# GpSimd joins the four score minima of a step, and evictions three and four carry on the minimum of one and two

## What is computed

```
q, k = fq_sym(q * scale, axis=-1), fq_sym(k, axis=-1)   # 8 bits per row
v = fq_sym(v, axis=2)                                   # 8 bits per column
attn = softmax(q @ k.T)                                 # per head, 1600 x 5776
attn = round(attn / s) * s, s = max(attn) / 255         # 8 bits per row
x = x + (attn @ v) @ Wp + bp
x = x + ffn(layernorm(x))                               # w13 (2816 x 512), w2 (512 x 1408)
```

## Time and profile before

| | us |
|---|---|
| median of three runs (1844.59 to 1848.37) | 1847.6 |
| the profiled execution | 1847.68 |
| its span | 1845.9 |
| VectorE busy | 1691.0 (92%) |
| TensorE matmuls busy | 1631.2 (88%) |
| ScalarE busy | 1391.7 (75%) |
| GpSimd busy | 1375.3 (75%) |
| evictions of 1536 and 1168 columns, mean of one | 1.81 and 1.42 |
| the join of the minima, mean of one | 0.16 |

### The profile page before, as it was taken

One profiled execution on the slowest core, in us unless ns is written; L12 is line 12 of the kernel. 1 busy time (PEld: TensorE's weight loads), 2 busy tenths in 40 slices (PEclk: granted clock), 3 DMA queues, 4 the chain that ended last, 5 costly groups with the idle time before them and its releaser, 6 DMA issues.

```text
span 1845.9 us, 41823 instructions
## 1 busy us (share of the span) xinstructions
PE 1631.2 (88%) x17032; PEld 1153.6 (62%) x17032; DVE 1691.0 (92%) x2670; ACT 1391.7 (75%) x1362; POOL 1375.3 (75%) x759
## 2 busy tenths in 40 slices
PE   7997899989888888888898898888889888789998
PEld 6884666666566666655566666555555555478876
DVE  6869999999999999999999999999999999986665
ACT  2446898888988898889888988897888888742232
POOL 1432789898879888888898889887898798753232
PEclk9999999999999999999999999999999999989999
DMA  5578988998899899989998998889888998732221
GB/s 175 193 224 201 209 187 177 184 196 166 181 186 198 176 193 184 187 164 177 191 200 177 181 196 170 158 158 181 168 169 157 205 185 160 166 116 45 67 58 47
DMA packets 851530, 309.96 MB, mean 168 GB/s; under 512 B 784966, under 2 KB 813964, under 8 KB 851212
## 3 DMA queue, kind: packets, MB, share of 16 engines
q1 hardware_dynamic: 851340, 307.29, 81.0%
HBM read 74.26 MB, written 39.59 MB: 62 GB/s over the span
## 4 chain that ended last, share of the span: by engine, by line
DVE 57%; PE 21%; issue 9%; POOL 7%; DMA 5%; ACT 1%; SPq 1%; POOLq 0%; DVEq 0%; ACTq 0%
DVE S L1295 51%; PE PS L876 5%; POOL PT L1529 5%; PE PK L913 3%; DMA PP<-Pr 3%; PE PS L743 2%; PE PK L682 2%; PE PK L684 2%; PE PS L711 2%; DVE MJ L1321 1%; PE PO L684 1%; DVE kam L1186 1%; PE PO L682 1%; DVE VMX L1190 1%; PE PO L762 1%
## 5 line engine op out<-in xcount | busy, mean ns | idle before, releaser
L1295 DVE TENSOR_SCALAR_CACHE_REDUCE S<-PS,SQN 128x1536 f32<-128x1536 f32 (+1 forms) x768 | 1283.2, 1714 | 20.5 <-PE PS L743 10.1
L1529 POOL CAST PT<-PP 128x3072 uint16<-128x3072 uint8 (+1 forms) x400 | 1048.5, 2650 | 223.6 <-DMA PP<-Pr 217.7
L1088 ACT ACTIVATE Pr<-S,MS 128x5888 uint8<-128x5888 f32 x200 | 1041.2, 5206 | 166.7 <-DVE MJ L1321 140.0
L743 PE MATMUL PS<-KT,QT 96*128 96x512 bf16 (+1 forms) x2496 | 633.4, 373 | 153.2 <-DVE S L1295 140.0
L762 PEld LDWEIGHTS PO<-VI,PT 128*128 128x128 f16 x9200 | 338.4, 96 | 199.6 <-issue 31.3
L743 PEld LDWEIGHTS PS<-KT,QT 96*128 96x128 bf16 (+1 forms) x2496 | 191.5, 99 | 364.9 <-DVE S L1295 131.1
L762 PE MATMUL PO<-VI,PT 128*128 128x32 bf16 x9200 | 356.3, 178 | 20.1 <-ACT AO L1038 9.7
L684 PE MATMUL PK<-CT,WG 128*128 128x128 f32 (+1 forms) x1288 | 212.7, 293 | 7.0 <-DMA CT<-ctxt 7.0
L682 PE MATMUL PK<-WG,CT 128*128 128x128 f32 (+1 forms) x1288 | 210.7, 293 | 6.3 <-ACT VF L949 3.7
L684 PEld LDWEIGHTS PK<-CT,WG 128*128 128x128 f32 x1288 | 169.1, 194 | 10.0 <-issue 7.8
L682 PEld LDWEIGHTS PK<-WG,CT 128*128 128x128 f32 (+1 forms) x1288 | 167.0, 192 | 8.5 <-issue 6.6
(11 more groups left out here) (156 smaller groups left out, 1538.0 us busy)
## 6 DMA issues: line engine op xcount, KB each, us to landing
CT<-ctxt SPq DMA_DIRECT2D x180, 256.0 KB, 3.2
k_rows<-KS SPq DMA_DIRECT2D x39, 512.0 KB, 4.0
q_rows<-QS SPq DMA_DIRECT2D x13, 512.0 KB, 4.6
W13F<-w13T SPq DMA_DIRECT2D x12, 352.0 KB, 3.7
PP<-Pr SPq DMA_TRANSPOSE x200, 6.0
XT<-x SPq DMA_DIRECT2D x12, 256.0 KB, 4.4
XR<-x SPq DMA_DIRECT2D x12, 256.0 KB, 3.3
base_rows<-XO SPq DMA_DIRECT2D x12, 256.0 KB, 3.3
```

The source lines that it names most:

```text
L743: last = pe.matmul(PS[n % 2][p0:p0 + r, f:f + w], QT[h % 3][0:PARTS * HD, q0:q0 + r], KT[h % 3][0:PARTS * HD, c * CHUNK + f:c * CHUNK + f ...
L1088: act.activation(Pr[i % 2].rearrange("p t q b -> p t b q"), S[i % 2].rearrange("p (t b q) -> p t b q", b=2, q=P), ACT.Exp, bias=MS[:, i % ...
L1295: v.tensor_scalar(S[i % 2][:, c * CHUNK:c * CHUNK + CW[c]], PS[n % 2][:, 0:CW[c]], neg_step, None, ALU.mult, ALU.min, accum_out=MN[:, i % ...
L1529: gp.tensor_copy(PT[i % 2][:, 2 * t0:2 * t1, :].rearrange("p (t b) q -> p t b q", b=2), PP[i % 2][:, t0:t1, :].bitcast(U8).rearrange("p t ...
```

## The change

The join leaves VectorE. Evictions three and four take as second scalar the minimum that eviction one or two left (`MN[:, i % 2, c - 2:c - 1]`), which seeds the running minimum, so that columns 2 and 3 of `MN` cover all four chunks. GpSimd takes the smaller of these two columns and adds ln 255 in one operation on 128x1, `offset(i)`, which signals `s_mx` in place of the join. Evictions three and four wait for the end of the eviction two before them. `offset(i)` is due at i + 0.25 in `todo`: ahead of `unpack(i - 2, 0)` at i + 0.3, and behind all that is due up to i + 0.25. It waits for all four evictions of step i.

```diff
-        MJ = sb("MJ", [P, NC_], F32)
...
                     v.wait_ge(M["s_qk"], n + 1)
 
-                    v.tensor_scalar(S[i % 2][:, c * CHUNK:c * CHUNK + CW[c]], PS[n % 2][:, 0:CW[c]], neg_step, None,
+                    if c >= 2:
+                        v.wait_ge(M["s_ev"], n - 1)
+                    least = MN[:, i % 2, c - 2:c - 1] if c >= 2 else None
+                    v.tensor_scalar(S[i % 2][:, c * CHUNK:c * CHUNK + CW[c]], PS[n % 2][:, 0:CW[c]], neg_step, least,
                                     ALU.mult, ALU.min, accum_out=MN[:, i % 2, c:c + 1]).then_inc(M["s_ev"], 1)
...
-                v.wait_ge(M["s_ev"], NC_ * (i + 1))
-
-                v.tensor_scalar(MJ[:, :], MN[:, i % 2, :], LN255, None, ALU.add, ALU.min,
-                                accum_out=MS[:, i % 2, 0:1]).then_inc(M["s_mx"], 1)
...
+            def offset(i):
+
+                gp.wait_ge(M["s_ev"], NC_ * (i + 1))
+                gp.tensor_scalar(MS[:, i % 2, 0:1], MN[:, i % 2, 3:4], MN[:, i % 2, 2:3], LN255, ALU.min,
+                                 ALU.add).then_inc(M["s_mx"], 1)
+
...
             todo += [(i + 2.3 + 0.4 * part, unpack, (i, part)) for i in range(NA) for part in range(NCAST)]
+            todo += [(i + 0.25, offset, (i,)) for i in range(NA)]
```

## The result

The changed kernel takes 1876.1 us (median; 1872.1 to 1878.7), the kernel before, run beside it on the same chip, 1847.9 us. The ratio is 1.0148, with a 95% interval of 1.0130 to 1.0166. The forecast was 1850 with a range to 1862. The median stands 4 us over this execution, the fastest of its kernel.

A forecast was written before the change was run, and what follows sets the result against it. VectorE's own instructions were taken to bound the attention phase; 46 us removed less 24 (seeds), 2, 4.5, 3, 6.5 (group changes), 2.5 (TensorE-paced steps) and 6 gave -2.5, so 1850 us; 8-in-10 range 1838 to 1862.

The forecast's parts named there:

- The tail: After the last step, casts waiting for the last offset delay w13's high parts and VectorE's last subtraction: 6 us lost.
- batches: Slots with two key operations on GpSimd (36 batches): only those four steps apart lose, 0.1 us each, 2 us.
- normalises: GpSimd's normalise, 2.1 us more in a slot, delays the exponential behind key operations: 4.5 us together.
- splits: Splits of w13 on GpSimd, 16 slots in two runs of eight, 6.98 against 6.69 us a slot: 3 us.
- TensorE's values for i-4 read casts made two slots before: hidden.: In plain slots, casts held behind the offset were claimed to cost TensorE's value products nothing.
- 2.7 late: Normalise behind two key operations (steps 54 and 104): exponential 2.7 us late, VectorE stalled 1.8 us.
- rival 1: GpSimd's queue costs more, through late exponentials: typically 8 to 12 us slower, 1858; chance 0.37 together with rival 3.
- It stalls VectorE up to 1.5 us: At three head-group changes, ScalarE's rounding of V waits for a cast behind an offset: 1 us each after partial absorption.
- Slack 0.9 us: In each step, how late the exponential could be before VectorE needs its score buffer: 0.9 us free.
- Rival 2: The slack absorbs GpSimd's queue: 10 us faster, 1837.5, or 1841 with half of the other terms; chance 0.25.
- Rival 3: Casts set the pace, so VectorE's time is worth nothing: some 1860 us; folded into rival 1, joint chance 0.37.
- The result hardly depends on the seed: Were seeds free on VectorE, other engines would take up the difference: 2 us faster instead of 2.5 slower.

The follow-up runs named there:

- the run without a join: Changed kernel with no GpSimd operation for the offset and no join anywhere, seeds kept, exponential taking column 3 of the minima as bias: 1831.5 us, ratio 0.9910.
- the run with the last offset moved: Changed kernel with only the last step's offset moved behind the two casts of step 197: 1869.6 us, ratio 1.0116.
- the run with the queue wait: Kernel before, join kept and no seeds, plus an unread one-column GpSimd operation at the offset's place with its wait: 1862.7 us, ratio 1.0077.
- a second operation: Changed kernel with another one-column GpSimd operation behind each offset, its result read by nobody: 1906.2 us, ratio 1.0323.
- the offset between the casts: Changed kernel with the offset of step i due at i + 0.5, between the two casts of step i-2: 1963.7 us, ratio 1.0624.
- the pair above: Changed kernel with normalises moved to slots without key operations (1865.1 us), and that with last offset and V casts moved too (1861.6 us), compared at steps 38 to 40.
- one copy on ScalarE: Changed kernel without GpSimd's operation; ScalarE copies the last minimum as bias ahead of each exponential, omitting the two-way minimum and ln 255: 1838.0 us, ratio 0.9943.

## Why the prediction was wrong

**What held.** The sign was right and the size wrong by a factor of ten: 2.5 us slower forecast, 28 measured. The removal (0.23 us a step: 6.92 with seeds and join, 6.69 with seeds alone) and the seeds (60 ns each, in the gapless evictions too) came out to the hundredth. The forecast took 5.8 us off VectorE's 22 for steps paced by transposes or by TensorE; 16.2 remain, and the steps of the run without a join are 16.3 us shorter in sum. The tail went by the path forecast, for 7.9 instead of 6 us.

**What failed is the queue, sized at 12.7 us in the steps** (batches 2, normalises 4.5, splits 3, the V casts 3.2 of the 6.5 for group changes). The step lengths of the changed kernel less those without a join, summed over the stretches around each cause, give 31.7: normalises (steps 26 to 37, 53 to 58, 81 to 88, 102 to 108, 131 to 137, 150 to 158) 12.4; V casts (38 to 52, 89 to 101, 138 to 149) 11.3; the two runs of splits (165 to 175, 183 to 192) 5.8; everything else 2.2. So -16.3 + 31.7 + 7.9 is 23.3, and with 0.2 for a later start of the first eviction the 23.5 of the spans. The split by cause is good to some 4 us only: the run with the last offset moved, whose steps are the same up to 199, gives the same 31.7 as 15.0, 7.6, 6.7 and 2.5. In the text's own steps:

1. "TensorE's values for i-4 read casts made two slots before: hidden." They weren't: 89.7 us of waits for casts in 99 places (22.5 in 16 before), and 45.8 us in 60 places for ScalarE's copies of value sums behind a late exponential (9.7 in 15 before). This is the step that failed first of all, an overlap that was taken for granted. The slot count followed two chains, casts and exponential to VectorE's buffer, and left out the one by which both reach TensorE, whose scores stand in program order behind the values. At step 57 I had 1.8 us (forecast for 54 and 104) and the trace shows 2.14 and 1.18.
2. The exponential "2.7 late": 3.5 at steps 55 and 105. The offset costs GpSimd 0.50 us, not 0.22: from the start of a key operation to the next cast it is 1.49 us with it (662.58 to 664.07) and such an operation alone takes 0.99 to the next start (572.77 to 573.76). The prediction named 0.5 as what would prove it wrong, and rival 1 decided from 0.35. The lower bound, the fill's 99 ns, was a bad neighbour; the operation with two inputs on 64 columns was the right one, and it too had been read without the time ahead of it.
3. "It stalls VectorE up to 1.5 us" at a V cast behind an offset: 3.3 us at step 46, but 0.87 us where the clock didn't fall behind it. The stall was rightly bounded; the half clock that can follow it was in no term. The long steps 83 and 133 (9.43 and 9.38 us) aren't the handshake for keys that the run with the queue wait has there: in the changed kernel VectorE waits 0.8 us for the exponential in each and TensorE 1.5 us for the copy of the sums behind it, as in step 57. They are the normalises "with one" key operation, which the text called mostly covered.
4. Slack 0.9 us, counted per step as if it were full again each time. 93 exponentials are over 1 us late.

**Rival 1** (the queue costs more, by the late exponential) had the right sign and mechanism, and too low a price: 8 to 12 us, "-19 at its worst", against 28. It held the exponential's queue and not TensorE's, nor the second charge that follows a TensorE wait. **Rival 2** is refuted by the counts above. **Rival 3** (the casts pace the kernel, VectorE's time is worth nothing) is half right: GpSimd holds 59% of the chain of the changed kernel, yet taking the seeds off VectorE still gave 10 of 24 us.

"The result hardly depends on the seed" held better than its number: taking the seeds out gave 10 us, where the text's two sums differ by 4.5.

**The clock.** No term of the sum held TensorE's clock. Between 170 and 1600 us the mean granted clock is 0.98 without a join, 0.97 in the changed kernel, 0.94 with a second operation and 0.93 with the offset between the casts. The falls seen above came behind waits of TensorE, but between kernels that are close the clock doesn't order them: with the queue wait it is 0.99, higher than before (0.98), and the kernel is slower. Three places show what falls cost: 2.5 us at step 46 and 1.2 at step 96 between the changed kernel and the same steps of the run with the last offset moved, and 2.8 in the pair above. For the whole an estimate is possible: in that stretch TensorE spent 79 us at half clock in the changed kernel and 65 without a join, and 15 us more at half clock is 7 us of its work, of the 31.7. What share of that reached VectorE isn't settled; no run here holds the clock and changes the waits.

In the Trainium skill, Perfetto Trace Analysis, GPSIMD Engine Instruction, start-to-start spacing is preferred to GpSimd's reported durations. By that rule the offset's 0.29 us was the wrong number to look at, and the trace agrees: 0.36 from its start to the next, 0.50 in all.

**Still open.** The changed kernel's other executions are 2 to 6.7 us above the profiled one. The clock goes with it: the four took 1872.1, 1874.1, 1878.2 and 1878.7 us at a mean granted clock of 0.970, 0.967, 0.963 and 0.961, and the eight with one copy on ScalarE reach from 1828.4 us at 0.982 to 1845.6 at 0.969. What decides whether a wait is followed by a fall, these runs don't show. So a difference of a few us between single profiled executions, step by step, isn't by itself an effect of the edit.

## What to carry to other kernels

Before a wait goes into an in-order queue, list everything behind it and follow each to every engine that reads it, one hop further than the engine you are watching: here casts and sums reached VectorE's pace through TensorE's program order. A tiny operation that others wait for does less harm on the engine that needs its result (ScalarE, ahead of the exponential: 25 us better than on GpSimd) than behind somebody else's long queue; here it still was no better than leaving it on VectorE. A stall of TensorE can be worth more than its length, since it may come out of it at half clock: 0.9 or 3.4 us for the same wait at step 46. And before two steps of two runs are compared, look at the clock of both.

## What the runs showed of the hardware

- A second per-partition scalar in an eviction costs VectorE 60 ns, in back-to-back evictions as in the pair of the earlier trace rows: 1.74 to 1.80 us for 1536 columns, 1.35 to 1.41 or 1.42 for 1168.
- A one-column GpSimd operation reports 0.29 us, as one on 64 columns does, and takes 0.36 to the next start and 0.50 out of the queue. The same size on ScalarE takes 0.20 to 0.30 us, and 0.24 to 0.33 where the next depends on it.
- TensorE fell to half clock (1.2 instead of 2.4 GHz) after waits of 0.72, 1.60 and 2.79 us. After the same waits it fell in one execution and not in another, twice: steps 38 to 40 (2.8 us longer) and step 46 (2.5 us longer).
- VectorE's widening of 512 columns to fp32r took 1.46 us without a join, 1.86 before, 2.75 in the changed kernel and 2.96 with the last offset moved. All four ended 0.28 us after the end of the GpSimd cast that was running when they started (before: cast to 1612.30, widening to 1612.58; changed: 1636.38 and 1636.66), so the time is what was left of the cast. The subtraction of two inputs of 2816 columns, 3.08 us by itself, ended 2.94 us after such a cast, 5.41 to 5.62 us in all. It goes the other way as well: with the last offset moved, the subtraction started first and took 3.09 us, and the cast that started 1.01 us into it took 4.68 instead of 2.74. In these tails whichever of the two started first went through, and the other waited.
